# Early keys of the second attention, and the ternary layer's transposes in fp32 with the rounding constant left in

## What is computed

```
x = x + tanh(g_xattn[0]) * L0_xattn(ctx, ctx, layernorm(x))     # 16 heads, exp features
x = x + tanh(g_ffn[0])   * sign-weight layer(layernorm(x))
x = x + tanh(g_xattn[1]) * L1_xattn(layernorm(x), ctx, ctx)     # k = ctx @ Wk + bk
x = x + tanh(g_ffn[1])   * L1_ffn(layernorm(x))                 # "ternary": bitlinear, gelu, bitlinear
x = x + tanh(g_xattn[2]) * L2_xattn(...)                        # keeps the top 64 of 77 scores
...

def bitlinear(x, W, b):
    w_scale = clip(mean(|W|), EPS)
    Wq = clip(round(W / w_scale), -1, 1) * w_scale
    x_scale = clip(max(|x|, axis=-1), EPS)
    xq = clip(round(x * (127 / x_scale)), -128, 127) * (x_scale / 127)
    return xq @ Wq.T + b
```

## Time and profile before

| | |
|---|---|
| runs | median 928.25 us, 927.47 to 928.56, 3 runs |
| profiled execution | 926.96 us, its span 925.2 us |
| PE busy | 807.2 us, 87% of the span |
| DVE, ACT, POOL busy | 668.1, 501.8, 540.9 us |
| mean granted clock of TensorE | 0.952 of full |
| first attention | about 20 to 146 us |
| middle part | about 146 to 300 us |
| third attention's dropping of scores (DVE) | from 293 us |

### The profile page before, as it was taken

How to read it: one execution, slowest core, us unless ns; L and a number is a source line. 1 busy time by engine, 2 the same in 40 slices (tenths; PEclk the granted TensorE clock), 3 DMA queues, 4 the chain that set the end, 5 groups by cost and what they waited for, 6 DMA issues and landing times.

```text
span 925.2 us, 19030 instructions
## 1 busy us (share of the span) xinstructions
PE 807.2 (87%) x5858; PEld 631.0 (68%) x5864; DVE 668.1 (72%) x2775; ACT 501.8 (54%) x1288; POOL 540.9 (58%) x730
## 2 busy tenths in 40 slices
PE   6899999998667477777888878999999999998898
PEld 4677767885445254545566668887788779987776
DVE  3888785789998999999999484454555552425887
ACT  3677764579885686888876522111121111226673
POOL 2565643676752788888767404454555555336883
PEclk9999999999899596999998889999999999999999
DMA  9100001000000055000000282222222224230001
GB/s 285 61 1 2 2 1 46 2 1 1 1 1 1 2 202 209 1 18 8 24 25 29 99 266 88 40 36 42 40 42 42 35 43 102 23 103 1 12 28 54
DMA packets 37790, 46.70 MB, mean 50 GB/s; under 512 B 4294, under 2 KB 33838, under 8 KB 37691
## 3 DMA queue, kind: packets, MB, share of 16 engines
q1 hardware_dynamic: 29211, 35.77, 11.4%
q0 software_dynamic: 8480, 9.72, 6.9%
HBM read 33.80 MB, written 11.68 MB: 49 GB/s over the span
## 4 chain that ended last, share of the span: by engine, by line
PE 56%; DVE 26%; POOL 5%; issue 5%; ACT 4%; DMA 2%; SPq 0%; DVEq 0%; POOLq 0%; ACTq 0%
PE ps L2755 11%; PE ps L2766 11%; DVE experts L1640 4%; DVE experts L1630 4%; PE ps L2248 3%; PE ps L2271 3%; DVE m L1625 3%; DVE m8b L1635 3%; PE ps L2235 2%; PE ps L2810 2%; PE ps L2784 2%; DVE mx L1622 2%; PE ps L2258 2%; PE ps L2166 2%; DVE sm L1563 2%
## 5 line engine op out<-in xcount | busy, mean ns | idle before, releaser
L1897 DVE COPY ptall<-experts 128x512 f32 x136 | 53.1, 431 | 94.4 <-PE ps L2755 62.1
L2755 PE MATMUL ps<-xnT,ptall 128*128 128x128 f32 x896 | 106.1, 277 | 0.0
L2755 PEld LDWEIGHTS ps<-xnT,ptall 128*128 128x128 f32 x896 | 103.8, 194 | 0.3 <-issue 0.3
L2766 PE MATMUL ps<-experts,wk 128*128 x448 | 102.0, 381 | 1.4 <-ACT xkeep L1251 1.4
L1241 ACT ACTIVATE wk<-ps 128x1024 f32<-128x1024 f32 x34 | 34.8, 1024 | 113.8 <-PE ps L2755 93.7
L2766 PEld LDWEIGHTS ps<-experts,wk 128*128 128x128 f32 x448 | 83.0, 190 | 16.9 <-issue 6.8
L765 POOL DMA_INDIRECT xn<-expert_in,rown x34 | 34.3, 1010 | 89.4 <-PE ps L2743 58.5
L681 POOL TENSOR_TENSOR experts<-experts,mx 128x616 f32<-128x616 f32 x32 | 39.1, 1223 | 51.4 <-DVE experts L1640 51.1
L598 POOL TENSOR_TENSOR experts<-experts,rden 128x616 f32<-128x616 f32 x32 | 38.8, 1216 | 47.4 <-DVE rden L1420 47.4
L790 POOL DMA_INDIRECT token_sum<-xkeep,dest x28 | 47.5, 1696 | 30.8 <-ACT xkeep L1251 22.4
L2166 PE MATMUL ps<-ones 128*128 128x256 bf16 x456 | 59.8, 288 | 5.8 <-POOL mone L553 5.8
(11 more groups left out here) (362 smaller groups left out, 2364.0 us busy)
## 6 DMA issues: line engine op xcount, KB each, us to landing
experts<-in_ew SPq DMA_DIRECT2D x16, 1024.0 KB, 11.4
x<-in_x SPq DMA_DIRECT2D x1, 2048.0 KB, 11.0
xkeep<-in_bw SPq DMA_DIRECT2D x2, 1024.0 KB, 7.2
expert_in<-xkeep SPq DMA_DIRECT2D x8, 256.0 KB, 4.1
x<-token_sum SPq DMA_DIRECT2D x8, 256.0 KB, 3.8
out<-x SPq DMA_DIRECT2D x7, 256.0 KB, 2.1
token_sum<-x SPq DMA_DIRECT2D x4, 256.0 KB, 2.5
token_sum<-x SPq DMA_DIRECT2D x1, 1024.0 KB, 4.4
```

The costliest lines, as they stand in the source:

```text
L1897: ins = nc.vector.tensor_copy(tilew[:, v, c, :], experts[:, bass.ds(e * EW + (c * FF + v * 512), 512)])
L2755: ins = nc.tensor.matmul(ps[j % 2][:, v, k * P:(k + 1) * P], tilew[:, v, c, k * P:(k + 1) * P], xTb[j % 3][:, c, :], start=c == 0, stop=c ...
L2766: ins = nc.tensor.matmul(bank(4)[:, 0:D], hidT[j % 2][:, k * P:(k + 1) * P], experts[:, bass.ds(e * EW + (E * EW + k * D), D)], start=k == ...
```

## The change

Two parts. First, the keys of the second attention are made inside the first attention, in banks 6 and 7, where `warm` was; for that the eight banks are emptied in another order (`EMPTIED`), and PE's first projections and scores wait for the banks they use, no longer for all eight. Second, the ternary layer keeps `MAGIC` in its numbers while they are turned: the transposes are fp32, and ACT takes `MAGIC` off when it copies them out of PSUM (`whole`). `mid_hidden_ints` and `mid_ints` go, `mid_quant` moves from ACT to DVE, the turned hidden rows take `ps[3]` (two banks), and the second matmul takes bank 1. `mid_values2` moves up by a step. The minimum with 127 is no longer taken. The first item of the third attention is scored in `ps[2]`, and the third (i = 2) waits for the last ternary sum.

```diff
-            for b in range(B):
+            for b in EMPTIED:                              # (0, 2, 3, 6, 7, 4, 5, 1)
...
             def lx_queries(b):
-                    pe.wait_ge(prep_v[0].sem, prep_v[0].past(8))
+                    pe.wait_ge(prep_v[0].sem, prep_v[0].past(3))
             def lx_scores(b, j):
+                    pe.wait_ge(prep_v[0].sem, prep_v[0].past(7))
...
+            def next_keys(j, part):
+                m, h = j // 2, j % 2
+                if j == part == 0:
+                    pe.wait_ge(s_w[2], 3 * 16)
+                    pe.wait_ge(prep_v[0].sem, prep_v[0].past(4))
...
+                ins = nc.tensor.matmul(bank(6 + h)[:, 0:HALF], w1k[:, part, m * P:(m + 1) * P],
+                                       ctxT[:, part, h * HALF:(h + 1) * HALF], start=part == 0, stop=part == CH - 1)
...
-                if k == 1:
-                    warm(5, 7)
...
-                    warm(12, 7)
+                    next_keys(2, 0)
+                    next_keys(2, 1)
...
-            def mid_hidden_ints(b, t):
-                nc.vector.tensor_scalar(hq[t], hmag[t], MAGIC, QB, ALU.subtract, ALU.min).then_inc(ghz, 1)
...
-                nc.vector.tensor_scalar(xq[p], xng[p], MAGIC, QB, ALU.subtract, ALU.min).then_inc(gq2, 1)
+                for t, quantised in enumerate((gqm, gq2)):
+                    nc.vector.tensor_scalar(xq[p][:, t, :], xng[p][:, t, :], sm[:, t, 1, b:b + 1], MAGIC, ALU.mult, ALU.add
+                                            ).then_inc(quantised, 1)
...
+            def whole(dst, src):
+                return nc.scalar.activation(dst, src, ACT.Copy, bias=-MAGIC)
...
-                copy(hT[t], bank(6).bitcast(bf16)).then_inc(ghc, 1)
+                whole(hT[t].rearrange("p (v n) -> p v n", v=2), ps[3][:, :, :]).then_inc(ghc, 1)
...
             def mid_flip_h(b, t):
-                pe.wait_ge(ghz, i + 1)
+                pe.wait_ge(ghq, i + 1)
...
-                    ins = nc.tensor.transpose(tb[:, j * P:(j + 1) * P], hq[t][:, j * P:(j + 1) * P], identb[:, :])
+                    ins = nc.tensor.transpose(ps[3][:, j // 4, j % 4 * P:(j % 4 + 1) * P], hmag[t][:, j * P:(j + 1) * P],
+                                              ident[:, :])
```

More of the change, by code:

```diff
@@ L891, in lx_out, with next_keys @@
                 copy(oT[b % 2][:, j, :], bank(6)[:, 0:S]).then_inc(ot_s[0].sem, 1)
+            def next_keys(j):
+                ac.wait_ge(k1p, j + 1)
+                nc.scalar.activation(key1[:, j // 2, (j % 2) * HALF:(j % 2 + 1) * HALF], bank(6 + j % 2)[:, 0:HALF],
+                                     ACT.Identity, bias=cols[:, 3 + j // 2:4 + j // 2]).then_inc(k1s, 1)
             for k in range(B + 2):
@@ L913, in _ @@
                     lx_exp(k - 1, 1)
+                if k == 1:
+                    next_keys(3)
                 if k < B:
@@ L979, in mid_norm_g @@
                 if b >= 2:
+                    ac.wait_ge(gqm, b - 1)
                     ac.wait_ge(gq2, b - 1)
                 post_norm(xng[p], rows2(b), rs_b[p], nm_b[p]).then_inc(gn, 1)
[L983 to L989, removed]
+            def whole(dst, src):
+                return nc.scalar.activation(dst, src, ACT.Copy, bias=-MAGIC)
             def mid_turned_g(b):
@@ L995, in mid_turned_g @@
                     ac.wait_ge(gh, TB * (b - 1))
-                copy(xqT[p].rearrange("p c s -> p (c s)"), bank(0)[:, 0:S].bitcast(bf16)).then_inc(gk, 1)
+                whole(xqT[p].rearrange("p c s -> p (c s)"), bank(0)).then_inc(gk, 1)
             def mid_gelu(b, t):
@@ L2186, in _ @@
             pe.wait_ge(prep_a[0].sem, prep_a[0].past(8))
-            for b in range(B):
+            for b in EMPTIED:
                 for g in range(GR):
@@ L2303, in _ @@
                 if k == 1:
-                    warm(5, 7)
+                    next_keys(3, 0)
+                    next_keys(3, 1)
                 if 0 <= k - 1 < B:
@@ L2312, in _ @@
                     lx_flip_p(k - 1, 0, 0)
-            def mid_keys1(j):
-                m, h = j // 2, j % 2
-                if j:
-                    pe.wait_ge(k1s, j)
-                for c in range(CH):
-                    ins = nc.tensor.matmul(bank(4)[:, 0:HALF], w1k[:, c, m * P:(m + 1) * P],
-                                           ctxT[:, c, h * HALF:(h + 1) * HALF], start=c == 0, stop=c == CH - 1)
-                ins.then_inc(k1p, 1)
             def mid_keys2(j):
@@ L2431, in mid_flip_g @@
                 freed(ak, k - 3)
-                tb = bank(0).bitcast(bf16)
-                for c in range(CH):
-                    for t in range(TB):
-                        ins = nc.tensor.transpose(tb[:, c * S + t * P:c * S + (t + 1) * P],
-                                                  xq[b % 2][:, t, c * P:(c + 1) * P], identb[:, :])
+                ins = flip(bank(0), xq[b % 2])
                 ins.then_inc(gf, 1)
```

93 lines of the change are left out of this document (52 added, 41 removed).

## The result

The changed kernel takes 919.96 us (median of 4 runs, 919.19 to 920.53), the kernel before beside it 928.4: ratio 0.9911, interval 0.9891 to 0.9931. That is 8.3 us less (6.4 to 10.1), where 7.3 was predicted. The profiled execution took 919.19 us with a span of 917.4, against 926.96 and 925.2; TensorE's mean granted clock is 0.957 instead of 0.952.

What follows compares the result with a forecast made beforehand. TensorE was taken to bound the first attention, ACT and VectorE the ternary layer's first step, VectorE the third attention. Terms of -2.0, -1.5 and -3.8 sum to -7.3 us: 928.25 becomes 920.9, given as 921.0; range 916.5 to 925.0.

Steps and rivals of the forecast that it cites:

- (e): Whole kernel: the author's own forecast, 918 to 923.5 us; chance 0.59.
- (b): Whole kernel: everything at its far end, with full clock in the ternary layer; -9 to -12 us, 917; chance 0.12.
- Term 1: First attention's start: projection and scores wait for fewer banks, start earlier, and the clock does not halve; -2.0 us.
- Term 2: Middle part's start: four key matmul calls leave TensorE, less 0.5 us for the moved `mid_values2`; -1.5 us.
- Term 3: Ternary layer: subtractions leave VectorE and quantisations leave ACT, shortening its steps; -3.8 us.
- The two full engines: Ternary layer's first step: ACT busy 10.71 and VectorE 10.39 us, relieved alike; 0.9 us taken there.
- I cost it at nothing: Ternary layer: 1.2 us more TensorE per step from fp32 transposes fits its room, costing nothing except at the end.
- the ring: Ternary layer's fifth step: as long as scaled, Gelu, largest, scale, `mid_magic`, scaled; no removed work, so 0 gain.
- (a): Ternary layer: other waits take over in each step, only the starts gain; -3.5 to -4.5 us, 924; chance 0.16.
- (c): First attention: without `warm` TensorE could stand at half clock, making it slower, 930 to 932 us; chance 0.06.
- (d): Whole kernel: gains swallowed by the DMA and a new third-item wait; within 1.9 us; chance 0.07.
- A difference behind it: Expert layer, behind the third attention: any change there would be something the prediction did not see; no size given.

Runs made afterwards that it cites:

- keys_only: Kernel before with only the first part: early keys and the new order of emptied banks; median 924.89 us.
- quant_act: Changed kernel with the two pieces of the input's quantisation put back on ACT, fp32 turns kept; median 922.42 us.
- longer_turns: Changed kernel with four of the eight fp32 turns of each hidden row tile done twice; median 923.11 us.
- half_turns: Changed kernel with only four of the eight fp32 turns for every hidden row tile but the first; median 919.55 us.
- order_only: Kernel before with only the banks' emptying order and relaxed waits changed, keys not moved and `warm` kept; median 925.61 us.
- after_again: Changed kernel run once more, unaltered, for a second profile; median 920.19 us.
- keys_behind: Changed kernel with the three key matmuls put behind the first scores, not ahead, and later keys one gap further; median 920.43 us.

## Why the prediction was right

**The number.** 921.0 was predicted and 919.96 measured, inside the range. The likeliest case (e) happened, with a part of (b) in it.

**Term 1** (-2.0) is -2.2 in the first profile and -1.9 in the second, both against the first profile of before, and -2.2 by the means of all profiles, but its working was not right. The order of the banks gives 2.8: the projection starts when its input is there, as predicted, 1.5 us earlier, and the return of the full clock gives not 0.6 but 1.5: 0.4 on the projection, 0.5 on five `warm` matmuls, 0.6 on the scores (less 0.2 in which VectorE is not ready yet). Against that, the step "three key matmuls come between projection and scores, and ACT's two exps run beside them" failed: VectorE waits 0.93 us for the scores behind them, and they cost 0.8. Two errors of about 0.8 cancelled; that was luck.

**Term 2** (-1.5) was mis-sized: 2.1 to 2.2 measured. The DMA's wait stayed as long and TensorE's wait of 1.72 went, both as predicted. The 0.5 us that I took off for the early `mid_values2` isn't there: keys_only, without that move, gains 2.2, and the two profiles after gain 2.1 and 2.2.

**Term 3** (-3.8) is 3.65 us by four profiles of each form, and 3.4 by the medians of the part alone. Its total is right and its working only in part. The first three steps fell by 2.6 us together for a predicted 2.5, but at the same clock only by 1.7: the first two bear the relief out (0.7 and 0.8 for 0.9 and 0.8), the third (0.2 for 0.8) doesn't. The two full engines also don't count alike in the first step: by quant_act the relief of VectorE alone gives 0.1 us there and ACT's the other 0.56; what ACT's alone would give, no run shows. Two more steps of the argument were wrong. "I cost it at nothing" of the longer turns was: 0.4 more of a turn costs 0.4 in the fourth and fifth step, as longer_turns and half_turns show from both sides, and 1.3 at the end by longer_turns alone, since ACT's Gelu stands behind the copy that waits for the turn; the ring as I wrote it left that out. At full clock throughout, the end is 1.15 us longer (16.98 against 15.83), not 0.3. And the profile of before was a lucky one: that 15.83 is 17.14 to 17.19 in the three other profiles with that layer. The longer turns cost time and the clock, which stays up where it used to fall, gives it back: some half of the 3.65 us is the clock's. Rival (b) had this mechanism, at a fifth of the chance of (e), so that the sum comes out at 3.65 for 3.8 is in good part luck. That TensorE's longer activity is the reason is only supported, by half_turns. One bound of the range was also mis-worked: if each step falls to 7.7, rows 7 give 8.2 us, not 5.5.

**The two rules of the Trainium skill** ("SBUF — State Buffer", "SBUF: two separate sides"; "TensorE: Matmul & The Clock Gate", "Part 4: PE-mode transpose"). The first spoke against the change through held quantisations: here none was held, all 16 took 321 to 350 ns. But what GpSimd ran beside them were operations of one or two columns, and in before only subtractions that began inside one of 512 or 616 columns were held (1.21 us at 224.96, 1.77 at 270.36), so this run doesn't decide it. By the second, longer transposes would not keep the clock up; in the layer's last step the nine profiles with full or longer fp32 turns have 1.00, the one with half of them and three of the four with bf16 ones 0.90, which speaks against it.

**The rivals.** (a), other waits taking over in each step, came true for the fifth step (0.2 us longer at full clock) and the end alone. (c), a clock at half without `warm`, did not happen: 1.00 from 24 to 225 us. (d), the new wait of the third item, is not seen: VectorE is busy all of the first 182.72 us from its first item on. "A difference behind it" was seen in the first pair of profiles; it sits ahead of the last item, and after_again has it no more.

## What to carry to other kernels

Before a gain or loss of 1 to 2 us is assigned to a stage, take a second profile of both kernels and look at the clock of each stretch: here one lucky profile halved a stage's apparent gain and its partner showed 1.6 us that the second one didn't, while single edits run alone agreed with the count within their intervals. An engine with room still costs what it is made longer, if another engine's queue waits for it with the next link of the ring behind. And where a bound engine's block begins, count its waits just ahead: 7.8 us of them were worth 5.8 to a change of order alone.

## What was not expected of the hardware

The granted clock of the same instructions differs from execution to execution: from the start of its fourth step on, the old ternary layer had a mean of 1.00, 0.96, 0.92 and 0.92, and took 1.4 to 2.3 us longer where it was below 1.00 (41.68 to 42.65 us against 40.32). Runs of one kernel spread with it: in longer_turns the five with a mean clock over the whole execution of 0.963 to 0.967 took 920.3 to 922.7 us, the five with 0.956 to 0.959 took 923.5 to 925.5. And a wait of TensorE of 2.1 us was enough at the start for the clock to be at 0.50 in what came next (in all three profiles with that wait), while with a wait of 0.7 to 0.8 us (order_only, keys_behind) it stayed at 1.00, in the one with `warm` behind it and in the other with scores and keys.
